# Another written order for attention and mixture, with stack loads issued step by step and the order behind the attention changed

## The reference

```
x = layernorm(x + channel_attention(x))          # 256 x 256 energies
x = layernorm(x + lora_mixture(x))               # 8 experts, top 2, F = 896
x = layernorm(x + causal_attention(x))           # 16 heads of 16, two matrices
x = layernorm(x + expert_mixture(x))             # 32 experts of 96, top 8 cut at a share of 0.8
```

## Time and profile before

| | us |
|---|---|
| median of the runs | 1507.35 |
| the runs | 1501.89, 1507.35, 1508.98 |
| the profiled execution | 1494.95 |
| its span, first to last instruction | 1493.2 |
| mean granted TensorE clock | 0.944 |

### The profile page before, as it was taken

One profiled execution on the slowest core, in us unless ns is written; L12 is line 12 of the kernel. 1 busy time (PEld: TensorE's weight loads), 2 busy tenths in 40 slices (PEclk: granted clock), 3 DMA queues, 4 the chain that ended last, 5 costly groups with the idle time before them and its releaser, 6 DMA issues.

```text
span 1493.2 us, 20335 instructions
## 1 busy us (share of the span) xinstructions
PE 1404.2 (94%) x7956; PEld 1002.5 (67%) x7956; DVE 926.9 (62%) x1779; ACT 622.9 (42%) x884; POOL 247.2 (17%) x341
## 2 busy tenths in 40 slices
PE   7899999999999989999999999999799999999995
PEld 6688788788787854344344344454687888888884
DVE  4655654754755677887887678853456545665454
ACT  3323322322322323565657466656243434434331
POOL 1300200200200011112112112221022222222221
PEclk9999999999999986898999699989899999999998
DMA  7000000000000575007005100000011111111110
GB/s 286 1 1 1 0 1 0 0 1 1 22 0 0 186 169 86 1 1 85 2 2 69 18 2 2 12 23 1 11 32 54 43 44 53 43 52 45 43 60 29
DMA packets 31833, 55.42 MB, mean 37 GB/s; under 512 B 6393, under 2 KB 13305, under 8 KB 31225
## 3 DMA queue, kind: packets, MB, share of 16 engines
q1 hardware_dynamic: 29688, 53.85, 14.4%
q0 software_dynamic: 2048, 0.27, 0.2%
HBM read 43.21 MB, written 10.49 MB: 36 GB/s over the span
## 4 chain that ended last, share of the span: by engine, by line
PE 77%; DVE 9%; ACT 4%; issue 3%; DMA 2%; POOL 0%; SPq 0%; POOLq 0%; DVEq 0%; ACTq 0%
PE ps L1327 51%; PE ps L1613 9%; PE ps L1537 8%; PE ps L1591 5%; DVE mpart L1109 2%; ACT probs L795 2%; DMA stack<-mrow 1%; PE ps L1380 1%; PE ps L1555 1%; PE ps L1334 1%; DVE mpart L1112 1%; PE ps L1622 1%; PE ps L1391 1%; DVE x L875 0%; DVE x2f L1046 0%
## 5 line engine op out<-in xcount | busy, mean ns | idle before, releaser
L795 ACT ACTIVATE probs<-ps 128x1024 f32<-128x1024 f32 (+3 forms) x320 | 272.5, 895 | 189.0 <-PE ps L1591 187.8
L1327 PE MATMUL ps<-xtd,gu 128*128 128x512 f32 x1152 | 285.0, 403 | 8.5 <-DVE x L1154 4.8
L1109 DVE TENSOR_REDUCE mpart<-ps 128x1 f32<-128x512 f32 x384 | 240.3, 684 | 59.5 <-PE ps L1537 58.3
L1327 PEld LDWEIGHTS ps<-xtd,gu 128*128 128x128 f32 x1152 | 217.4, 192 | 59.6 <-issue 10.4
L1537 PE MATMUL ps<-stack 48*128 48x512 f32 (+3 forms) x832 | 211.1, 402 | 16.6 <-DVE mpart L1109 7.9
L1537 PEld LDWEIGHTS ps<-stack 48*128 48x128 f32 x832 | 110.5, 199 | 145.5 <-DVE mpart L1109 85.9
L1327 PE MATMUL ps<-ma,b 128*128 128x512 f32 x672 | 166.6, 396 | 11.8 <-DVE x2f L1058 7.4
L1591 PE MATMUL ps<-stack 50*128 50x512 f32 (+3 forms) x640 | 160.0, 443 | 11.9 <-ACT probs L795 6.0
L1613 PE MATMUL ps<-probs,vaug 128*32 128x512 f32 (+3 forms) x1280 | 165.7, 594 | 3.1 <-ACT probs L795 2.5
L1327 PEld LDWEIGHTS ps<-ma,b 128*128 128x128 f32 x672 | 125.3, 188 | 44.8 <-DVE x2f L1058 10.5
L1327 PEld LDWEIGHTS ps<-dn,hpart 128*128 128x128 f32 x1152 | 143.9, 189 | 5.2 <-DVE hpart L875 0.9
(11 more groups left out here) (175 smaller groups left out, 1601.0 us busy)
## 6 DMA issues: line engine op xcount, KB each, us to landing
gu_raw<-in_wgu SPq DMA_DIRECT2D x48, 256.0 KB, 2.6
stack<-qk_dram SPq DMA_DIRECT2D x72, 128.0 KB, 8.7
qk_dram<-qk_out SPq DMA_DIRECT2D x16, 512.0 KB, 3.8
dn_raw<-in_wdn SPq DMA_DIRECT2D x48, 128.0 KB, 2.7
stack<-qk_dram SPq DMA_DIRECT2D x48, 64.0 KB, 2.4
x<-in_x_tm SPq DMA_DIRECT2D x4, 512.0 KB, 5.0
xt_in<-in_x_fm SPq DMA_DIRECT2D x1, 2048.0 KB, 13.2
out<-x SPq DMA_DIRECT2D x4, 512.0 KB, 3.4
```

What stands on the lines that cost most here:

```text
L795: act.activation(probs[:, (2 * r + p) % 4, :, off:BLK], banks(bank)[:, :, off:BLK], ACT.Exp, scale=float(HD) ** -0.5).then_inc(exp_done.se ...
L1109: ins = dve.tensor_reduce(part[:, p, qt % TPB, 2 + kb:3 + kb], ps[:, bank, :], AX_X, ALU.max)
L1327: mm = pe.matmul(out, lhs(i), rhs(k), start=first and n == 1, stop=last and n == todo, **more)
```

## The change

- `ORDER` is another string with the same letters in the same numbers (1066: 512 `u`, 320 `S`, 159 `P`, 16 `M`, 15 `O` and so on). The banks follow from it. Near its start the norm of block 3 (`N`) stands before the fourth projection; near its end `r`, `s`, `f`, `k`, `m`, and the third `w` stand later, and the last `e` stands before the last `S`.
- `load_group` waits, before each two of its 24 transfers, for the scores of one more step: group 1 for steps 3 to 14, group 2 for steps 40 to 51, group 3 for steps 80 to 91. Before, all 24 were issued in a row.
- Behind the string, `head` of the last round stands before the `gu` of (0, 1, 0), and `resC` of block 3 before the first `down`.
- The last two `down` entries are replaced. Block 2's share of the last two steps is summed first and signalled (`last`, `summed`), then block 3's. DVE adds block 2, adds block 3, takes the statistics of both, and then normalises both.
- ACT runs one exponential on one column (`warm`) ahead of its walk of the plan.

```diff
--- before.py
+++ after.py
@@ -53,16 +53,16 @@
 
 
 ORDER = (
-    "qqTLRqqVNuuuTuuuVuuquVMuuTuuuquuquuquuVuSuuSuSuuSuPuuuPSuuuSuuMuuuPuuuSuuuuuuSuSuuuuuuuuuuPuuuuuuSuuuSSuuPuSuS"
...
-    "PSuSSuSuuPwdPMeerSSOSwSPSaPSSbSPSsfkSPcSSPSSPSSPSSPSSmPSSPSSPSdPSSSPSSPSSPxe"
+    "qqTLRqNqVuuTuuuVuuTuuVMuuuquuquuuquuuSquuuVuuSuuSSuuuPuuPSuuuuSuuuPuuMuuuSuuuuSuuSuSuuuuPuuuuuuuuuuuSSuPuSSPuS"
...
+    "uPSPSSuuuSdPPMeeSSOSSPSaPSSbrSPSSPSSPScsSPSSPSSfPSSPSSPkSSPSSmPSSPSSwdxPPSeS"
 )
 
 
@@ -150,15 +150,15 @@
     values(len(steps) - 1)
     pair("gu", (0, 0, 1), 0)
     one("out", left[0])
+    mark("head", left[0])
     pair("gu", (0, 1, 0), 2)
-    mark("head", left[0])
     pair("turnO", NB - 1, 6)
     pair("gu", (0, 1, 1), 4)
     pair("proj", NB - 1, 6)
+    mark("resC", NB - 1)
     mark("down", (0, 0))
     mark("whi", 3)
     pair("gu", (0, 2, 0), 4)
-    mark("resC", NB - 1)
     pair("gu", (0, 2, 1), 6)
     mark("down", (0, 1))
     mark("whi", 4)
@@ -175,7 +175,8 @@
                 else:
                     mark(kind, key)
             pair("gu", (hf, j, tb), next(slots))
-        mark("down", ((i - 1) // JT, (i - 1) % JT))
+        if i < 2 * JT - 1:
+            mark("down", ((i - 1) // JT, (i - 1) % JT))
         if i + 2 < 2 * JT:
             mark("whi", i + 2)
         if (hf, j) == (1, 0):
@@ -185,8 +186,12 @@
                 mark("statD", b)
             if (hf, j) == (1, 3 + 2 * b):
                 mark("normD", b)
-    mark("down", (1, JT - 1))
-    mark("acc", 1)
+    for b in range(2, NB):
+        mark("last", b)
+        mark("sum", b)
+    for kind in ("statD", "normD"):
+        for b in range(2, NB):
+            mark(kind, b)
     return steps, rounds, units, closes, plan
 
 
@@ -218,6 +223,7 @@
         triexp = at("triexp", [P, P], BF16)
         iota = at("iota", [P, E1], F32)
         half_neg = at("half_neg", [P, TPB], F32)
+        warm = at("warm", [P, 1], F32)
         ln_stats = at("ln_stats", [P, 2, TPB, 6], F32)
         ln_mv = at("ln_mv", [P, 2, TPB, 2], F32)
         ln_var = at("ln_var", [P, 2, TPB], F32)
@@ -459,6 +465,7 @@
         h_hi = sig("h_hi", hjt)
         h_lo = sig("h_lo", hjt)
         down1 = sig("down1", hj)
+        summed = sig("summed", range(2, NB))
         acc_read = sig("acc_read", bb)
         stored = sem("stored")
 
@@ -537,14 +544,16 @@
                                   qk_dram[2 * which + g // 2, part, GH * HD * (g % 2):GH * HD * (g % 2 + 1), BLK * b:BLK * (b + 1)]
                                   .rearrange("(i a d) t -> a d i t", a=2, d=HD)[par]).then_inc(done, 16)
 
-            def load_group(g, which, done):
-                for c, part, par in parts_of(which):
+            def load_group(g, step):
+
+                for n, (which, (c, part, par)) in enumerate((w, rows) for w in (1, 0) for rows in parts_of(w)):
+                    sp_.wait_ge(*st_ready.after((step + n, HP - 1)))
                     lo = 64 * par + HD * c
                     for i in range(HP):
                         r0 = GH * HD * (g % 2) + HD * (2 * i + par)
                         sp_.dma_start(stack[lo:lo + HD, g % 2, which, :, i, :].bitcast(F32),
                                       qk_dram[2 * which + g // 2, part, r0:r0 + HD, :].rearrange("d (n t) -> d n t", n=NB)) \
-                            .then_inc(done, 16)
+                            .then_inc(stack_in[g % 2], 16)
 
             def ones_rows(i):
                 for par in range(2):
@@ -568,8 +577,7 @@
             sp_.wait_ge(*v_ps.after(NB - 1))
             sp_.wait_ge(*qk_ps.after((NB - 1, 1)))
             ones_rows(1)
-            for which in (1, 0):
-                load_group(1, which, stack_in[1])
+            load_group(1, 3)
             sp_.dma_start(wo_raw[:, :, :], wo_d).then_inc(wo_in, 16)
             sp_.dma_start(wg1_raw[:, :, :], wg1_d).then_inc(wg1_in, 16)
 
@@ -580,9 +588,7 @@
             for n in range(3):
                 raw_weights(n)
             for g in range(2, NG):
-                sp_.wait_ge(*st_ready.after(((g - 1) * per_group - 1, HP - 1)))
-                for which in (1, 0):
-                    load_group(g, which, stack_in[g % 2])
+                load_group(g, (g - 1) * per_group)
             for n in range(3, len(hj)):
                 sp_.wait_ge(*wd_lo.after(hj[n - 3]))
                 raw_weights(n)
@@ -690,8 +696,6 @@
                     moe_weights_lo(key)
                 elif kind == "statD":
                     rstd("D", key)
-            for b in range(2, NB):
-                rstd("D", b)
 
 
         @block.scalar
@@ -821,6 +825,8 @@
                     act.wait_ge(*down1.after(hj[n - 2]))
                 copy(hpart[:, n % 2, tb, 0, :], hfull[:, tb, :]).then_inc(h_hi.sem, 1)
 
+            act.wait_ge(pool_const, 1)
+            act.activation(warm[:, :], half_neg[:, 0:1], ACT.Exp)
             for kind, key, bank in plan:
                 if kind == "v":
                     values_in(key, bank)
@@ -1244,14 +1250,9 @@
                 dve.wait_ge(*h_hi.after(key))
                 low(hpart[:, n % 2, tb, 1, :], hfull[:, tb, :], hpart[:, n % 2, tb, 0, :]).then_inc(h_lo.sem, 1)
 
-            def accumulated(hf):
-                dve.wait_ge(*down1.after((hf, JT - 1)))
-                for b in range(2 * hf, 2 * hf + 2):
-                    xb = x[:, TPB * b:TPB * (b + 1), :]
-                    dve.tensor_tensor(xb, tiles(2 * (b % 2)), xb, ALU.add).then_inc(acc_read.sem, 1)
-                    if hf:
-                        dve.wait_ge(*acc_read.after(b))
-                        layer_norm("D", b)
+            def add_mixture(b):
+                xb = x[:, TPB * b:TPB * (b + 1), :]
+                dve.tensor_tensor(xb, tiles(2 * (b % 2)), xb, ALU.add).then_inc(acc_read.sem, 1)
 
             where = {}
             for kind, key, bank in plan:
@@ -1309,8 +1310,14 @@
                 elif kind == "gu":
                     hidden_parts(*key, bank)
                 elif kind == "acc":
-                    accumulated(key)
+                    dve.wait_ge(*down1.after((0, JT - 1)))
+                    for b in range(2):
+                        add_mixture(b)
+                elif kind == "sum":
+                    dve.wait_ge(*summed.after(key))
+                    add_mixture(key)
                 elif kind == "statD":
+                    dve.wait_ge(*acc_read.after(key))
                     statistics("D", key)
                 elif kind == "normD":
                     normalise("D", key)
@@ -1679,6 +1686,18 @@
                                  j == 0 and a % 2 == 0, j == JT - 1, skip_group_check=True)
                 mm.then_inc(down1.sem, 1)
 
+            def last_down(b):
+
+                tb = b % 2
+                for j in (JT - 2, JT - 1):
+                    n = hj_no(1, j)
+                    pe.wait_ge(*h_lo.after((1, j, tb)))
+                    for t in range(TPB):
+                        mm = product(tiles(2 * tb)[:, t, :],
+                                     [(lambda i: hpart[:, n % 2, tb, i, P * t:P * (t + 1)], lambda k: dn[:, n % 3, k, :])],
+                                     False, j == JT - 1, skip_group_check=True)
+                mm.then_inc(summed.sem, 1)
+
             pe.wait_ge(wqkv_ready, 1)
             for kind, key, bank in plan:
                 if kind == "v":
@@ -1722,6 +1741,8 @@
                     gates_ups(*key, bank)
                 elif kind == "down":
                     down(*key)
+                elif kind == "last":
+                    last_down(key)
 
 
 def kernel(**inputs):
```

More of the change, by code:

```diff
@@ L55 @@
 ORDER = (
-    "qqTLRqqVNuuuTuuuVuuquVMuuTuuuquuquuquuVuSuuSuSuuSuPuuuPSuuuSuuMuuuPuuuSuuuuuuSuSuuuuuuuuuuPuuuuuuSuuuSSuuPuSuS"
-    "PuSuSPuSSMuPuuuuuSSuuPuuuSuuPuuSSuuSuPOPuuSuSSuuSuuPuSuuSPuSuSuuuuuPuSSuuuuPuSuuuuuPuuSSuSuuuPSOuSPSuSuPMuSSuu"
-    "PuSuSuPuPSuSSuSuPSuSuuuPuuSSuPuuSuPSuSuSuuPuSSuuMuuPSSPuSSuuPSSuuPuSuSPuuSuSPuuSSuMPSuSuuOuPuSuSPuSSuuuuuPuSPS"
-    "SuuuSuPuSuSPSuuPSuuOuuPuSuSSSuPuuuuSPuSSuuuMSuPuSuuSuPuSPuSuOSuuSuPSSuuuPuSuPuSSuuPSuuuSPuuuSSuPuSSuuuuPuSuuuu"
-    "SuPSuuSuuSuPSuuuSPuSuuSuPSSuPMSuSOPuuSSPSuuPSSuuSPuSuSuuuPSSuPSMuuuuSPuSSuuuuPuuuuSSOuPuuuPSuSuuSuSuPuuuySSPuS"
-    "uuSPuuuSuSPuuSSuuPSuuSuPSMuSPuuSuuuSPuSPuuSuSSuuPuSSuOuPuSuSuPSuPSSuPSSuuuSuPuSSPOuuSSPSMSPuSuuuuPSuuSuuSPuuPu"
-    "SSuSuYSuuPuSuSPuuuSSuPuuuSuuuuPuSSuuuuuSPSuuuuSPuuPSuuuSuuSSPuSSuuPSPMuuSuuuSSPSSOuPPuSuSSuSuuPSuuSuPuSuSPuSuP"
-    "SuuSuuSMPuuuuSSPSuSuuuPSSuuPuuuSuPuSSuOuuSuPSuSuuPuuSSPuMSSuuPuuSSuuuPSuSuPuuPSSuuuuuSSuPOuuuSSPuuSuSuPPSuSSuS"
-    "uuPSuuSMPuSuSOPuSSuuPuuuuSSPuSSuuuuPSSuuPuSuPSuuauSPuSuuOSbSPuSuaSuuwPuSPSSuPcSuuSuuPSuuudbuuSPuSSPuuSuSuSuuPc"
-    "PSuSSuSuuPwdPMeerSSOSwSPSaPSSbSPSsfkSPcSSPSSPSSPSSPSSmPSSPSSPSdPSSSPSSPSSPxe"
+    "qqTLRqNqVuuTuuuVuuTuuVMuuuquuquuuquuuSquuuVuuSuuSSuuuPuuPSuuuuSuuuPuuMuuuSuuuuSuuSuSuuuuPuuuuuuuuuuuSSuPuSSPuS"
+    "uuPSuuuuMuPuSuuSSOSuuPSuuSuPuuuSPSSuSuPSuuSuOuuuPuuuSSuPuuuSuSuPSuSuuuuPuSuPuuSuuuSSuuPuuPuuSuuSuuSuPSuSuMSuuP"
```

(8 more changed lines are left out.)

## The result

| | before | after |
|---|---|---|
| median, us (runs side by side, 4 each) | 1508.16 | 1457.55 |
| lowest to highest | 1501.89 to 1516.53 | 1450.42 to 1465.10 |
| profiled execution | 1494.95 | 1450.42 |
| its span | 1493.2 | 1448.7 |
| its mean granted clock | 0.944 | 0.965 |

The ratio after to before is 0.9691 [0.9643, 0.9739]: faster by 47 us by the ratio and 51 by the medians, where 20 were forecast and 1472 us was the low end. Beside the later experiments the kernel before ran far more often, with medians of 1501.4, 1500.6, 1501.1 and 1502.0 us (11, 11, 23 and 23 executions, 1484 to 1521 us), and the changed kernel again at 1459.15 (6 executions, 0.9714 [0.9664, 0.9764]).

A forecast was written before the change was run, and what follows sets the result against it. PE was taken to bound the kernel, through waits, granted clock and the tail. From the median, 1507.35 - 20.2 (3.5 + 9.5 + 1.3 + 0.9 + 5) = 1487 us; own range 1480 to 1495, 8 in 10 within 1472 to 1505.

The forecast's parts named there:

- The order itself, taken at 0: Attention: the new string only moves waits; not costable from the trace, between -6 and +8 us, taken at 0.
- Paced loads, -5 us: Attention: spreading the stack loads saves 0.9 us of waits, plus -5 us by clock, a fifth of filling both long pits.
- The wait of the second round's maxima: Attention, near 550 us: PE's wait for the row maxima's transfers stays at 1 to 2 us despite paced loads.
- rival (4): Attention: slower, 1524 us; the second round's maxima get a shorter lead, PE waits 6 us, two more clock pits; chance 0.07.
- Behind the attention, -9.5 us: Stretch after the attention: moving head and resC earlier removes two PE waits; 7.5 to 11.4 us depending on clock.
- The end, -3.5 us: Program's end: summing block 2 first shortens the tail by 4.0 us, less some store overlap; -3.0 to -4.0.
- The warm exponential, -1.3 us: First scores: ACT's table load moves ahead of the first projection's copy and is hidden there; between 0 and -1.6 us.
- The base: Whole kernel: forecast counted from the median 1507.35 us, since the profiled execution lay 12.4 us under the median.
- (2): Attention: rival in which both long clock pits are filled, -42 us in all, 1465 us; chance 0.10.
- (1): Attention: rival in which pacing buys nothing, the pits come anyway, only the ends count, -14.3, 1493 us; chance 0.20.
- (3): Attention: rival in which the new order draws one more pit of 28 us, +13.4, about 1506 us; chance 0.15.
- the marks set: Signs of being right or wrong: the attention's clock and idle time, waits at moved steps, tail length, maxima transfers under 5 us.

The follow-up runs named there:

- e2: The kernel before with only the new string: 1494.34 us, ratio to before 0.9895.
- e4: The changed kernel with the old string put back: 1477.71 us, ratio to before 0.987.
- e9: The changed kernel run again, unaltered: 1459.15 us, ratio to before 0.9714.
- e1: The kernel before with only the paced loads: 1494.6 us, ratio to before 0.9978.
- e3: The changed kernel with the stack loads issued in one go again: 1465.79 us, ratio to before 0.9751.
- e5: The kernel before with only the code behind the string changed (head, resC, last two steps): 1477.81 us, ratio to before 0.9879.
- e8: The kernel before with the new string and the paced loads, without the ends and the warm exponential: 1476.72 us, ratio to before 0.9842.
- e7: The changed kernel without the warm exponential: 1462.85 us, ratio to before 0.9689.
- h2: The changed kernel with the old string, except letters 296 to 461 from the new one: 1463.03 us, ratio to before 0.9747.
- j4: The kernel before with letters 296 to 461 from the new string, nothing else changed: 1503.8 us, ratio to before 0.9984.
- j2: The changed kernel with the old string, except letters 365 to 461 from the new one: 1486.02 us, ratio to before 0.9894.
- j3: The changed kernel with letters 296 to 461 put back to the old string's: 1469.5 us, ratio to before 0.9785.

## Why the prediction was wrong, step by step

**What bounds the kernel** held: PE carries it, and time went by waits, clock and tail.

**"The order itself, taken at 0"** is the step that failed. Its reason, that "the letters move waits only", is false: with the new string PE idled 1.7 to 3.4 us more in the attention (four pairs of profiles), and still the string is worth 7 us alone by the medians, 15.8 by the ratio (e2: 1.05% of 1501), and 18.5 us within the changed kernel (e4 against e9), all of it clock. The bound of -6 was drawn from idle time alone. The old profile already showed PE busy for 27.55 of 28 us at half clock, so the clock was not following idle time alone, and what set it should have been priced as unknown: a new string could take away any of the falls, down to all of the 54 us lost in the attention, and add falls of 13.4 us each, which is a far wider range than -6 to +8.

**Paced loads, -5 us.** The size was about right (3 us by e1's ratio, 6 by e3 against e9, neither clear of zero by the times alone), the mechanism was not. I gave them 0.9 us of waits and the rest as clock, "both long pits lie directly behind those two waits or around them". e1 and e4 have paced loads and falls all the same, near 540 us in both, later at 858 and at 840 us, and with the changed ends the pacing moves lost by +2.9 (e5 to e4) and +0.4 (e3 to e9). Only with the old ends does lost fall, by 9 us (before to e1) and 14 (e2 to e8). What the paced loads do in every pair is take 3.8 to 7.1 us of PE's idle time, a term that I had at 0.9; under the new string 4.8 us of it are the waits for the row maxima.

**The wait of the second round's maxima.** I had it stay at 1 to 2 us; it is gone. The unpaced kernels e2 and e3 show it at 5.4 and 4.1 us: rival (4) had the mechanism right, 6 us, and had it wrong that the paced loads would not relieve it.

**Behind the attention, -9.5 us.** Right mechanism, undersized: 12.5 us, in e5 11.2. Both waits behave as worked out (0.81 and none). What was mis-sized is the clock: I took about half of the 3.9 us that hung on it, and all of it came back, 0.9 on the turn and 0.7 + 2.4 on the two runs of `gu`. Another 0.9 us came in the first `gu` of the stretch, 12 matmuls in 4.52 rather than 5.46 us, which I had not costed: the fall behind the third router logits, 6.8 us long in before, is 3.4 us long there. That the logits lower the clock, as the prediction has it, fits the profiles: a fall comes with the first two in all 18.

**The end, -3.5 us** (4.0 before the stores). It was 4.5: the last normalising ended 7.9 us behind the last matmul (8.3 expected), and the end of the program 12.0 us behind it (12.5 expected). The stores, 1.4 us apart, gave nothing back.

**The warm exponential, -1.3 us**: nothing measured, and by the traces nothing gained, since the load stands on the chain in front of the first copy, while in e7, which has the new string without the warm exponential, the wait of 1.61 us is gone anyway. The second half of its claim holds: no table load stands beside the first scores.

**The base.** The profiled execution of before lay 12.4 us under the median, and I forecast from the median 1507.35. On 23 executions it is 1501 to 1502. This is 6 us of error that runs the other way: against 1501.5 the forecast would have been 1481 and the changed kernel's 1459 would have been missed by 22.

**The rivals.** (2) named 1465 us, nearest to the result, by filling both pits through the loads. The size of clock is right (lost went from 95 to 60), the cause is not: under the old string the same loads leave the pits. (1), pacing buys nothing for the clock, is right about the cause by e4 and e3, and about the sum it is wrong, since it too has the order at 0. (3), one more pit of 28 us, is what h2's and j4's profiles show for a mixed string, and it did not happen here.

Of the marks set: the mean clock of the attention rose from 0.90 to 0.93, idle was 30.5 us (28 to 42 allowed), no wait stood over 1.5 us at the two moved steps, and one transfer of the maxima, at 5.8 us, was over the 5 that I had named.

## What to carry to other kernels

When PE's busy time with the same instructions changes, look at the granted clock before any wait: here all that a rewritten order gave was matmuls at the full clock, with no less idling. Price a reordering of a kernel with stretches at half clock by what those stretches hold, on both sides, and measure it on many executions, since a fall can come in some and not in others. Moving a short DVE step ahead of work that PE needs less gave back its wait here, and also the clock of the matmuls behind it.

## What the runs showed of the hardware

- The clock falls while PE is busy: 54.58 of 55 us at a clock of 0.50 in j4, behind 11 us in which PE idled 0.6, and 10.2 us in before behind 5.5 us in which it idled none. By lost, the low clock takes 94 to 96 of before's 1500 us, time idled at a low clock included, and 61 of the changed kernel's 1459. The Trainium skill, "TensorE: Matmul & The Clock Gate", section "HAM oscillation — how this bites in real kernels", ties such falls to gaps in which PE is idle. Right ahead of the fall at 994.9 us in before PE works for 5.5 us without a gap, so the trace doesn't bear idle gaps out as the only cause.
- The falls stick to places of the instruction order more than to times: letters 327 to 329 in before, e1, e4, e5, j2 and j3, at 673 to 687 us, and the router logits of letter 1004 in all 18 profiles, from 969 to 1013 us. Yet later ones depend on what came hundreds of letters earlier.
- The kernel before scatters from 1484 to 1521 us, and most of that is lost clock: an execution of 1489 us lost 77, one of 1521 us 117.
- A row maximum's four small transfers land in 1.6 us, and in up to 10.8 us beside or right behind 24 loads of 128 KB issued in a row on another queue.
